# A decoder layer on one core: the dense layer from three fp16 products instead of one fp32 product, with its weights split during the first attention

## The reference

```
x = x + attention1(layernorm(x))      # 32 query heads, 8 key heads, sign weights, no mask
x = x + block2(layernorm(x))          # read, causal attention of 16 heads of 16, write, read, gated product with ctx, write
x = x + dense(layernorm(x))
def write(res, y):                    # twice in block2
    out, low = split(y @ wod.T)       # 256 and 8 columns
    A_B = y @ wab.T + wab_b           # 112 columns
    delta = softplus(low @ du.T + du_b)
    A_bar = exp(delta * -softplus(A_logit)); ...
    return hs * A_full + out * B_full
def dense(x):                         # gate picks an adapter for each of 8 blocks of 128 tokens
    return x @ kernel + bias + (x @ A_eff.T) @ B_eff.T + (x @ A_shared.T) @ B_shared.T
```

## Time and profile before

| | us |
|---|---|
| median of 3 runs | 1153.41 (1146.45 to 1155.86) |
| the profiled execution itself | 1156.17 |
| its span on the core | 1154.4 |
| TensorE busy | 953.4 (83%) |
| VectorE busy | 651.2 (56%) |
| ScalarE busy | 431.1 (37%) |
| GpSimd busy | 346.8 (30%) |

### The profile page before, as it was taken

One profiled execution on the slowest core, in us unless ns is written; L12 is line 12 of the kernel. 1 busy time (PEld: TensorE's weight loads), 2 busy tenths in 40 slices (PEclk: granted clock), 3 DMA queues, 4 the chain that ended last, 5 costly groups with the idle time before them and its releaser, 6 DMA issues.

```text
span 1154.4 us, 16645 instructions
## 1 busy us (share of the span) xinstructions
PE 953.4 (83%) x5482; PEld 555.2 (48%) x5482; DVE 651.2 (56%) x1354; ACT 431.1 (37%) x786; POOL 346.8 (30%) x308
## 2 busy tenths in 40 slices
PE   1259999799999999687795799947589999999987
PEld 1236544344445445255563444425456656656644
DVE  6752136476677675356665656232476577568551
ACT  4841112466556657112221245520322423324220
POOL 4530000565666657600000033320221222222110
PEclk9999999799999999899987566556699999999997
DMA  6653273321232231103247453010000011010000
GB/s 255 223 211 113 77 229 122 75 71 55 69 87 69 54 87 43 56 2 90 58 107 258 92 121 75 33 45 11 1 1 19 19 37 30 7 36 28 10 27 37
DMA packets 58831, 87.69 MB, mean 76 GB/s; under 512 B 16336, under 2 KB 34560, under 8 KB 57504
## 3 DMA queue, kind: packets, MB, share of 16 engines
q1 hardware_dynamic: 58352, 80.96, 23.3%
q10 hardware_dynamic: 432, 6.12, 1.4%
HBM read 61.42 MB, written 25.23 MB: 75 GB/s over the span
## 4 chain that ended last, share of the span: by engine, by line
PE 55%; DVE 12%; issue 11%; DMA 8%; ACT 6%; SPq 3%; POOL 3%; DVEq 0%; POOLq 0%; ACTq 0%; PEldq 0%
PE psum L1346 8%; PE psum L1651 7%; PE psum L1392 5%; PE psum L1637 5%; PE psum L1423 4%; DMA q_op<-q_scr 3%; PE psum L1435 3%; PE psum L1604 3%; PE psum L1446 3%; PE psum L1510 3%; PE psum L1593 2%; DMA kr<-q_scr 2%; PE psum L1709 2%; DMA qk_scr<-hi_st 2%; PE psum L1641 2%
## 5 line engine op out<-in xcount | busy, mean ns | idle before, releaser
L1007 DVE TENSOR_REDUCE m_neg<-psum 128x1 f32<-128x512 f32 x256 | 165.8, 682 | 73.6 <-PE psum L1392 73.6
L765 ACT ACTIVATE region_x<-psum 128x512 f32<-128x512 f32 x256 | 143.2, 597 | 105.3 <-PE psum L1423 104.0
L609 POOL TENSOR_TENSOR region_p<-region_x 128x2048 f32<-128x2048 f32 x32 | 146.6, 4583 | 69.5 <-ACT region_x L765 37.7
L1651 PE MATMUL psum<-region_a,c_o 128*128 128x512 f32 x256 | 117.6, 601 | 0.0
L1392 PE MATMUL psum<-kr,q_op 96*128 96x512 f32 x176 | 79.3, 462 | 10.9 <-DMA q_op<-q_scr 10.1
L1346 PE MATMUL psum<-region_x,region_w 128*128 128x512 f16 x320 | 73.4, 386 | 1.2 <-DVE region_p L995 1.2
L1423 PE MATMUL psum<-q_op,kr 98*128 98x512 f32 x176 | 71.3, 412 | 0.2 <-ACT region_x L765 0.2
L1709 PE MATMUL psum<-ynT,region_w 128*128 128x128 f32 x512 | 63.7, 289 | 7.6 <-ACT ynT L907 7.6
L1651 PEld LDWEIGHTS psum<-region_a,c_o 128*128 128x128 f32 x256 | 46.5, 192 | 48.5 <-issue 48.5
L1435 PE MATMUL psum<-region_x,v_g 128*32 128x512 f32 x512 | 68.6, 611 | 0.0
L1709 PEld LDWEIGHTS psum<-ynT,region_w 128*128 128x128 f32 x512 | 62.1, 204 | 13.4 <-ACT ynT L907 13.4
(11 more groups left out here) (215 smaller groups left out, 1726.9 us busy)
## 6 DMA issues: line engine op xcount, KB each, us to landing
q_op<-q_scr SPq DMA_DIRECT2D x33, 256.0 KB, 3.9
region_p<-in_x SPq DMA_DIRECT2D x16, 512.0 KB, 3.4
q_scr<-kr SPq DMA_DIRECT2D x24, 256.0 KB, 2.3
region_w<-in_wT SPq DMA_DIRECT2D x4, 1280.0 KB, 5.4
region_a<-in_wT SPq DMA_DIRECT2D x4, 1280.0 KB, 7.2
qk_scr<-hi_st SPq DMA_DIRECT2D x64, 64.0 KB
region_a<-in_kern ACTq DMA_DIRECT2D x1, 4096.0 KB, 18.4
out<-region_w SPq DMA_DIRECT2D x8, 512.0 KB, 2.6
```

The source lines that it names most:

```text
L609: pool.tensor_tensor(pair_sum[:, n], prob_a[:, 2 * n], prob_a[:, 2 * n + 1], ALU.add).then_inc(pair_ready, 1)
L765: act.activation(prob_a[:, kt, j, :], psum[:, (0, 4, 5)[(16 * k + n) % 3], :], ACT.Exp, scale=A_SCALE).then_inc(p_ready, 1)
L1007: dve.tensor_reduce(m_neg[:, k % 3, n:n + 1], psum[:, 1 + (16 * k + n) % 3, :], AX_X, ALU.max, negate=True).then_inc(s_max, 1)
L1651: pe.matmul(psum[:, 4 + h, :], hT_f[:, c, :], kern[:, c, h * 512:(h + 1) * 512], start=(c == 0), stop=False)
```

## The change

The fp32 dense product becomes three fp16 products: the state is split into fT_hi and fT_lo, the weights, times 64 (F_GAIN), into a high and a low half, and hi by hi, hi by lo and lo by hi are summed; the factor is taken out in finish.

- **Weights.** They are split in 16 pieces of 512 columns, one in each step of the first attention. SyncE loads a piece into w_st (load_kern, 256 KB), ScalarE rounds it (kern_hi, after part 12), VectorE forms the rest (kern_lo, after part 14), SyncE stores both halves to kern_scr in DRAM (store_kern, 128 KB each). The one DMA that loads the dense weights later reads kern_scr, of the same 4 MB. The three buffers take the place of v_x, whose memset moves behind the first attention; two memsets of kr and the mask move behind the second block's rstd.
- **Adapters.** gate_a is multiplied by 64, a_eff is split into a_hi and a_lo (so 16 stores instead of 8), the shared adapter is split on GpSimd during the second attention. The adapter product is made turned, 24 fp16 products with the weights on the array's 64 columns, so that the copy, the turning and a semaphore fall away.
- **Bias.** It is a row of lora_bt against a constant row of axT, and no longer part of rows; finish is one pass.
- **Low-rank columns.** The products of the writes have 376 columns and include them; ScalarE copies 8 columns out (low_rank), TensorE turns them (turn_low), ScalarE copies them again (low_turned).
- **State.** VectorE forms fT_lo in two subtractions (dense_lo) ahead of the last part of the first write.
- **Head.** Semaphores are merged where one can do for two.

```diff
...
+            sp.wait_ge(c_ready, 6 + R4)
             for b in range(NT):
-                sp.dma_start(a_scr[b], a_eff[:, b].rearrange("p c r -> p (c r)")).then_inc(lora_stored, 16)
+                for n, part in enumerate((a_hi, a_lo)):
+                    sp.dma_start(a_scr[n, b], part[:, b].rearrange("p c r -> p (c r)")).then_inc(lora_stored, 16)
...
+            def load_kern(i):
+                sp.dma_start(w_st.unsqueeze(1), kern_in[:, ds(i, 1), :]).then_inc(w_moved, 16)
+
+            def store_kern(t, k):
+                i = t * 3 + k
+                wait_apart(sp, (w_lo_ready, i + 1))
+                for n, part in enumerate((w_hi, w_lo)):
+                    sp.dma_start(kern_scr[n, :, ds(i, 1), :], part.unsqueeze(1)).then_inc(w_moved, 16)
+
+            sp.wait_ge(lora_stored, 16 * (2 * NT + 2))
+            load_kern(0)
             load_qk(0, 2)
             load_max(0, 1)
+            store_kern(0, 0)
+            load_kern(1)
             load_qk(0, 3)
             load_max(0, 2)
+            store_kern(0, 1)
+            load_kern(2)
             with sp.Fori(0, A_ROUNDS) as t:
                 for k in (2, 3, 4):
                     load_qk(t, k + 2)
                     load_max(t, k + 1)
+                    store_kern(t, k)
+                    load_kern(t * 3 + k + 1)
                     if k == 3:
                         sp.dma_start(ctx_parts[:, ds(t, 1), :], d["ctx"].rearrange("p w k n -> p (w k) n")[:, ds(t, 1), :]).then_inc(xw_loaded, 16)
             sp.dma_start(wqkv, d["wqkv"].rearrange("p o k n -> p (o k) n")).then_inc(xw_loaded, 16)
             load_max(0, NI - 1)
+            store_kern(0, NI - 2)
+            load_kern(NI - 1)
             sp.wait_ge(vg_ready, NI)
             sp.dma_start(read1, d["read1"]).then_inc(xw_loaded, 16)
             sp.wait_ge(den_done, 2 * NI + 2)
             load_x(0, 0)
             load_x(1, 1)
             load_max(0, NI - 1)
+            store_kern(0, NI - 1)
...
             pool.wait_ge(pv_done, 4 + QT * NI)
-            for r in (32, 96):
...
+            pool.wait_ge(w_moved, 48 * NI)
+            pool.memset(v_x, 1.0).then_inc(made, 1)
+            for i in range(NT):
                 pool.wait_ge(l_step, 5 * i + 5)
-                pool.tensor_tensor(rstds[:, ds(i, 1)], ves[:], minus_half[:, 0:1], ALU.pow).then_inc(l_rstd, 1)
+                pool.tensor_tensor(rstds[:, i:i + 1], ves[:], minus_half[:, 0:1], ALU.pow).then_inc(l_rstd, 1)
+                if i == 1:
+                    pool.wait_ge(l_rstd, 2)
+                    for r in (32, 96):
+                        pool.memset(kr[r:r + 32, :].bitcast(F32), 1.0).then_inc(made, 1)
+                    pool.wait_ge(made, 22)
...
+            def kern_hi(t, k):
+                act.wait_ge(w_moved, 48 * (t * 3 + k) + 16)
+                act.activation(w_hi, w_st, ACT.Copy, scale=F_GAIN).then_inc(w_hi_ready, 1)
...
+                    if n == 12:
+                        kern_hi(t, k)
...
+            def low_turned(k, i):
+                act.wait_ge(W["w_mm"][k], 2 * i + 2)
                 act.activation(low[k], psum[0:DR, 2 * k + 1, 0:P], ACT.Copy).then_inc(W["low_ready"][k], 1)
...
+            dve.wait_ge(lora_loaded, 16 * (2 * R4 + 2))
+            dve.tensor_scalar(gate_a, gate_a, F_GAIN, None, ALU.mult).then_inc(c_ready, 1)
             dve.wait_ge(trig_done, 4)
+            for r in range(R4):
+                dve.wait_ge(lora_ready, r + 1)
+                dve.tensor_tensor(a_lo[:, :, :, r * R8:(r + 1) * R8], psum[:, r, :].rearrange("p (c b r) -> p b c r", c=KC, b=NT),
+                                  a_hi[:, :, :, r * R8:(r + 1) * R8], ALU.subtract).then_inc(c_ready, 1)
...
+            def kern_lo(t, k):
+                dve.wait_ge(w_hi_ready, t * 3 + k + 1)
+                dve.scalar_tensor_tensor(w_lo, w_st, F_GAIN, w_hi, ALU.mult, ALU.subtract).then_inc(w_lo_ready, 1)
...
+                    if n == 14:
+                        kern_lo(t, k)
...
+            def dense_lo(i):
+                dve.wait_ge(fT_ready, 2 * i + 2)
+                for h in range(2):
+                    dve.tensor_tensor(fT_lo[:, 4 * h:4 * h + 4, :], psum[:, 6 + h, :].rearrange("p (c n) -> p c n", c=4),
+                                      fT_hi[:, 4 * h:4 * h + 4, :], ALU.subtract).then_inc(fT_lo_ready, 1)
...
             def finish(i):
                 dve.wait_ge(f_mm, i + 2)
                 dve.wait_ge(out_stored, 16 * i + 16)
-                o3 = out_t.rearrange("p (h n) -> p h n", h=2)
-                dve.tensor_tensor(o3, psum[:, 4:6, :], rows[:, slice(*ROWS["bias"])].rearrange("p (h n) -> p h n", h=2), ALU.add).then_inc(o_step, 1)
-                dve.wait_ge(o_step, i + 2)
-                dve.tensor_tensor(out_t.unsqueeze(1), out_t.unsqueeze(1), x1[:, ds(i, 1), :], ALU.add).then_inc(out_ready, 1)
+                dve.scalar_tensor_tensor(out_t.rearrange("p (h n) -> p h n", h=2), psum[:, 4:6, :], 1.0 / F_GAIN,
+                                         x1[:, ds(i, 1), :].rearrange("p o (h n) -> p (o h) n", h=2), ALU.mult, ALU.add).then_inc(out_ready, 1)
 
             def round_(i, u, first, second, dense, done):
                 if done and not first:
                     finish(i - 3)
+                if dense and not first:
+                    dense_lo(i - 2)
...
+            pe.wait_ge(c_ready, 6)
...
+            pe.wait_ge(c_ready, 6 + R4)
...
+            def dense_hi(h, part):
+                for c in part:
+                    for w in range(2):
+                        pe.matmul(psum[:, 4 + h, :], fT_hi[:, c, :], kern[:, w, c, h * 512:(h + 1) * 512], start=(c == 0 and w == 0), stop=False)
+
+            def dense_lo(h, part):
+                for c in part:
+                    pe.matmul(psum[:, 4 + h, :], fT_lo[:, c, :], kern[:, 0, c, h * 512:(h + 1) * 512], start=False, stop=False)
...
                     products(0, yT, write1, 2, range(2))
-                    low_products(0, yT, write1, 2)
                 if second:
                     pe.wait_ge(W["hn_ready"][1], 2 * i)
-                    products(1, mlpT, write2, KC, range(2))
+                    products(1, mlpT, write2, KC, range(1))
+                if first:
+                    turn_low(0, i)
+                if second:
+                    products(1, mlpT, write2, KC, range(1, 3))
                 if first:
                     deltas(0, i)
                 if second:
-                    products(1, mlpT, write2, KC, range(2, KC))
+                    products(1, mlpT, write2, KC, range(3, KC))
                 if dense:
                     pe.wait_ge(xf_ready, i - 1)
                     turn(6, h_out, KC, fT_mm)
                 if second:
-                    low_products(1, mlpT, write2, KC)
+                    turn_low(1, i - 1)
                 if dense:
                     pe.wait_ge(fT_ready, 2 * i - 2)
-                    pe.wait_ge(lo_loaded, 32 * i - 32)
-                    pe.wait_ge(o_step, i - 1)
+                    pe.wait_ge(lo_loaded, 48 * i - 48)
+                    pe.wait_ge(out_ready, i - 1)
                     for c in range(KC):
-                        mm = pe.matmul(psum[:, 5, 0:R2], hT_f[:, c, :], lora_at[:, c, :], start=(c == 0), stop=(c == KC - 1))
-                    mm.then_inc(ax_mm, 1)
+                        for w in range(2):
+                            pe.matmul(psum[0:R2, 5, 0:P], lora_at[:, c, w, :], fT_hi[:, c, :], start=(c == 0 and w == 0), stop=False)
                 if second:
                     deltas(1, i - 1)
                 if dense:
-                    dense_products(range(0, 6))
+                    dense_hi(0, range(KC))
+                    pe.wait_ge(fT_lo_ready, 2 * i - 2)
+                    for c in range(KC):
+                        mm = pe.matmul(psum[0:R2, 5, 0:P], lora_at[:, c, 0, :], fT_lo[:, c, :], start=False, stop=(c == KC - 1))
+                    mm.then_inc(axT_mm, 1)
+                    dense_lo(0, range(0, 3))
                 if first:
                     pe.wait_ge(W["hn_ready"][0], 2 * i + 2)
                     turn(6, h_mid[u], KC, h2T_mm)
...
-                    wait_apart(pe, (ax_ready, i - 1))
-                    pe.transpose(psum[0:R2, 5, P:2 * P], ax, ident[:]).then_inc(axT_mm, 1)
-                if dense:
-                    dense_products(range(6, 8))
+                    dense_lo(0, range(3, KC))
...
                 if dense:
                     pe.wait_ge(axT_ready, i - 1)
-                    dense_products(range(8, 12))
+                    dense_hi(1, range(KC))
...
                 if dense:
-                    dense_products(range(12, 13))
+                    dense_lo(1, range(0, 5))
...
                 if dense:
-                    dense_products(range(13, 16))
+                    dense_lo(1, range(5, KC))
                     for h in range(2):
-                        mm = pe.matmul(psum[:, 4 + h, :], axT, lora_bt[0:R2, h * 512:(h + 1) * 512], start=False, stop=True)
```

(1 more changed line is left out.)

170 lines of the change are left out of this document (94 added, 76 removed).

## The result

The changed kernel takes 1224.45 us (median of 4 runs, 1221.99 to 1232.7), the kernel before beside it 1154.63: ratio 1.063, 95% interval 1.056 to 1.071. It is slower, as forecast, and 24 us above the predicted 1200. The profiled execution has a span of 1220.3 us, 65.9 more than before; this difference is taken apart here.

What follows compares the result with a forecast made beforehand. The prediction took the first attention to be bound by its operand loads, the rounds by a loop through several engines. Terms 38 + 6 + 20 + 2 - 18 = +48 gave 1201 at the median, predicted 1200, range 1163 to 1235.

Steps and rivals of the forecast that it cites:

- signs: What would show the forecast in the profile: among others operand waits 50 to 60 us, steps 19.5 to 21.5, rounds 39.4.
- The load term: First attention: 13 operand loads issued behind the subtraction wait and three DMAs, 2.9 us each, +38; ctx in four, +6.
- The clock: First attention: TensorE's waits of about 4 us make its clock fall once in each of 13 steps, 1.5 us each, +20.
- GpSimd beside VectorE: First attention: contention on shared SBUF interfaces could delay the subtraction, each load up to 1 us later; within the upper bound.
- Edges: Start, last steps of the first attention, moved memsets, bias rows and adapter preparation: small gains and losses, together +2 us.
- The rounds: Dense rounds: TensorE gives up 5.6 us, the loop takes 1.7 in each of six; with later savings -18 us.
- the middle state comes only 0.2 us sooner: Dense rounds: decays start 0.8 us sooner, but two VectorE subtractions ahead of their use leave the middle state 0.2 sooner.
- the price of the subtractions: Dense rounds: VectorE's two subtractions of the turned state, 0.65 us each, right ahead of what uses the decays.
- The last two rounds: End of the kernel: round 8's exponential no longer waits for the adapter product, -2.5 us; the last round saves 5.5.
- The clock holds: Rival in the first attention: loads come late but TensorE's clock stays up, without the 20 us: 1181 us; chance 0.2.
- The stores find their data early: Rival in the first attention: subtraction ready before the last shifted product, DMAs in SyncE's waits: 1137 us; chance 0.11.
- It cancels: Rival: short wait for the subtraction, three issues cost 1.6 us a load, clock holds: +7, 1160 us; chance 0.09.

Runs made afterwards that it cites:

- e6: Changed kernel with 12 more TensorE products in each of 13 steps, ahead of its wait for the operand loads: 1205.17 us.
- e5: Changed kernel with its three DMAs per step kept, but copy and subtraction only in the first step, so no wait for a subtraction: 1162.35 us, ratio 1.006.
- e10: Changed kernel with ScalarE's copy and VectorE's subtraction of a piece earlier in the step, SyncE's order unchanged: 1188.17 us, ratio 1.030.
- e8: e2 without VectorE's two subtractions per round, their products taking the high half of the state: 1142.76 us, ratio 0.990.
- e3: Changed kernel with SyncE's subtraction wait, stores and piece load behind both the next operand loads and the row loads: 1187.68 us, ratio 1.037.
- e2: Changed kernel with SyncE's subtraction wait, stores and piece load behind the next operand loads, ahead of the row loads: 1146.16 us, ratio 0.995.
- e9: e2 with twelve more low-by-low fp16 products at the end of each round that has a next one: 1137.44 us, ratio 0.986.
- e1: Changed kernel without the weight splitting in the first attention, dense weights filled from another fp16 array: 1162.98 us, ratio 1.009.
- e4: Changed kernel keeping copy, subtraction and SyncE's wait, without stores and all but the first piece load; dense weights filled as in e1: 1201.39 us, ratio 1.046.
- e7: e2 with eight more low-by-low fp16 products at the end of each round that has a next one: 1139.61 us, ratio 0.988.

## Why the prediction was right, and where it was off

Right were the sign, the stage, the order on SyncE and the range (1163 to 1235). Of its signs three were missed: TensorE's waits for operands were 69.8 us and not 50 to 60, the steps 23.0 us and not 19.5 to 21.5, the rounds 40.9 us and not 39.4. The forecast's own sum was +48 for this execution, measured +66; the 18 us between them are 13 in the first attention, 9 in the rounds, and -4 at the edges.

- *The load term, 2.9 us and 0.5 for ctx (+38 and +6).* Part by part it holds. The subtraction took 0.68 us; the wait alone makes a full-clock step 17.84 us instead of 17.0; the DMAs behind it take SyncE 1.8 us (1.6 forecast). e6's full-clock steps give 3.2 us for the load. For ctx e5 gives 1.7 us a piece, forecast 1.5.
- *The clock, 1.5 us once per step (+20, 0 to 39).* This is the term that was mis-sized: 22.6 - 20.2 = 2.4 us a step, 31 us in 13, an estimate that takes the steps behind ctx to lose as much. I had the price of a fall from a step with a 1.55 us wait, where TensorE stayed at 1.2 GHz for 2 us; after waits of 4 us it stayed there for 6 us in many steps. These 11 us are most of the 13 that the stage is off; 42 for the loads, 7 for ctx and 31 for the clock make 80, measured 77. The Trainium skill's rule ("TensorE: Matmul & The Clock Gate", HAM oscillation), that a kernel waiting for a DMA at each tile falls to the half clock at each, is borne out: in the eight steps from 319.57 to 502.13 us the granted clock was 0.92 or lower every time.
- *GpSimd beside VectorE*, up to 1 us a load: didn't come, and wasn't put to the test. The subtraction took 0.68 us at 335.43, and GpSimd's long addition began only at 335.86; in e10 it took 0.63 to 0.84, again mostly ahead of or behind that addition. The rule on shared interfaces in the Trainium skill's "GPSIMD Engine Reference" (Specifications) bears on the rounds: there the operation on the decays, 0.96 us before, took 2.00 us, and 2.50 in e8.
- *Edges, +2.* The start came 4.4 us late, which the kernels with the same code there show to be its own scatter; the two stages behind the first attention were 6.4 us shorter, in the second attention with the clock at 0.69 where it had been 0.60 before. The change doesn't explain this: in the kernels above, which all have it, the second attention takes 90.3 (e3) to 102.2 us (e2, with the clock at 0.60).
- *The rounds, 1.7 us each (-18 in all).* The step that failed is "the middle state comes only 0.2 us sooner". In the round from 1043.10 it comes at 1061.18, 18.1 us after the round's start; in the earlier trace rows 17.3; in e9, with the clock held, 16.7. TensorE's longer wait at the start of a round lets its clock fall; the write's products then run slow, and VectorE waits for them. VectorE's timeline has it; before, the same addition began at 975.90, 5.2 us into the round, and here it begins 5.9 us into it:

```profile
1048.98 0.42 DVE L1275 TENSOR_TENSOR region_w<-psum,rows 128x256 f32<-128x256 f32 x1 [0.79 <-PE psum L1725]
```

  ScalarE's decays were to come 0.8 us sooner. Its timelines in the changed kernel and in e9:

```profile
1055.74 0.84 ACT L929 ACTIVATE region_w<-region_w 128x768 f32<-128x768 f32 x1
```

```profile
984.59 0.84 ACT L929 ACTIVATE region_w<-region_w 128x768 f32<-128x768 f32 x1
```

  They are done 13.5 us into the round, before 13.2, and 12.0 in e9: copies ahead of them wait for TensorE's turning of the dense block's state, which is late when the clock is low. From there to the state it is 4.6 us, before 4.1, so the price of the subtractions was about right (0.5 us, forecast 0.6), though e8 shows no gain without them.

  I had charged the clock in the first attention and forgotten it in the rounds, where the change takes work from TensorE just as well. With the clock held, e9's 39.1 us a round against the forecast 39.4 show that the rest of the step was right. The last two rounds gave 5.1 of the 9.2 us, forecast 8: at the start of the first of them TensorE waits 2.76 us, before 0.64, and the 16 products behind it take 8.17 us where they took 5.21.
- *Rivals.* "The clock holds" (1181) fell: e6 shows what it would be worth. "The stores find their data early" (1137) isn't what the changed kernel does; e2, which takes the stores out of the loads' way by their order, takes 1146. "It cancels" would have needed both a short wait and a clock that holds.

What stays open: why the issues of e1's and e4's substitute take so long (their 512-byte pieces are argued, not shown), what sets the moment at which the clock falls, why the start and the second attention scatter, and why e4's rounds take 380.9 us, 6 less than the changed kernel's.

## What to carry to other kernels

A DMA queue in program order is a chain: a store that waits for its data must not stand ahead of a load that the next step needs; behind it, the same stores were nearly free here (6.0 us a step became 0.2). When a change takes work from TensorE or makes it wait, price the clock of what follows as well as the wait, and price it from waits as long as the new ones. Where the time taken from TensorE only opens a wait, filling it with products can pay: it brought 9 us here, e9 beside e2.

## What the runs showed of the hardware

- TensorE's clock follows more than the last wait: in e4 after a wait of 2.5 us it stayed at 1.00 (308.17 to 311), after the next one, of 1.96 us, it was at 0.78 in the mean of 2.1 us, and after one of 4.4 us at 0.50 for 6.7 us; in the kernel before it fell after 1.55 us. In the changed kernel's rounds the clock fell after the same wait of 2.85 us, in turn about 1.4 us behind its end and already within it.
- More products made kernels faster: 12 more a step saved 19 us (e6), 8 or 12 more a round 7 or 9 (e7 and e9 beside e2).
- The same VectorE operation on 768 columns took 0.96 us (before the change, at 983.89), 1.25 (e9), 2.00 (changed kernel) and 2.50 (e8), each time beside GpSimd's product, which took 2.50, 1.84, 1.73 and 1.72 us: where VectorE's was short, GpSimd's was long.
- 512 KB right ahead of the operand loads in the queue let the last of these land after 5.7 to 6.2 us instead of 4.0 to 4.4 (5.0 in the first step), and made the step 1.7 us longer at full clock (e5), while two stores and a load, 512 KB together and the last issued 1 us ahead of the operand loads, cost nothing.
